# Attention on one core: the transposes of a head's sums stand behind the next head's second key block

## The reference, cut to what matters

```python
x = inputs.reshape(B, T, NUM_HEADS, HEAD_DIM).transpose(0, 2, 1, 3)
q = x * rotation_params[None, :, None, :]
k = x * entangle_params[None, :, None, :]
attn_scores = jnp.einsum('bhid,bhjd->bhij', q, k) / sqrt(16)
out = jnp.einsum('bhij,bhjd->bhid', softmax(attn_scores), x)
...
x = x + layernorm(attention(layernorm(x)))
x = x + layernorm(token_mixing_ffn(layernorm(x)))
x = x + layernorm(linear_attention_block(layernorm(x)))
x = x + layernorm(quantised_ffn(layernorm(x)))
```

## Time and profile before

| | |
|---|---|
| time, median of 3 runs | 3713.15 us (3712.55 to 3713.18) |
| the profiled execution: span | 3718.8 us (its own time is given only as this span) |
| TensorE matmul busy | 3322.9 us, 89% |
| ScalarE busy | 2477.6 us, 67% |
| VectorE busy | 1495.2 us, 40% |
| GpSimd busy | 214.5 us, 6% |
| TensorE's mean granted clock | 0.958 |
| DMA | 178.49 MB, mean 48 GB/s |

### The profile page before, as it was taken

One profiled execution on the slowest core, in us unless ns is written; L12 is line 12 of the kernel. 1 busy time (PEld: TensorE's weight loads), 2 busy tenths in 40 slices (PEclk: granted clock), 3 DMA queues, 4 the chain that ended last, 5 costly groups with the idle time before them and its releaser, 6 DMA issues. The chain is left out here.

```text
span 3718.8 us, 54135 instructions
## 1 busy us (share of the span) xinstructions
PE 3322.9 (89%) x18048; PEld 1368.4 (37%) x18049; DVE 1495.2 (40%) x3462; ACT 2477.6 (67%) x2634; POOL 214.5 (6%) x183
## 2 busy tenths in 40 slices
PE   1999999999999999999999966658888888889996
PEld 0222222222222222222222224435555666665664
DVE  5233211212201202202201026665677777765664
ACT  1998998998998998999999962223333333333332
POOL 0000000000000000000000001111111111111100
PEclk9999999999999999999999987879999999999998
DMA  6111111101101101101100011221111221110110
GB/s 208 62 36 35 55 32 37 51 29 44 52 31 40 46 31 48 48 30 48 39 31 31 31 26 51 74 59 49 46 51 51 62 68 51 51 48 33 45 35 23
DMA packets 122866, 178.49 MB, mean 48 GB/s; under 512 B 40016, under 2 KB 97616, under 8 KB 122320
## 3 DMA queue, kind: packets, MB, share of 16 engines
q1 hardware_dynamic: 122576, 174.75, 14.8%
HBM read 107.62 MB, written 67.11 MB: 47 GB/s over the span
## 5 line engine op out<-in xcount | busy, mean ns | idle before, releaser
L368 ACT ACTIVATE probs<-ps 128x1024 f32<-128x1024 f32 x2048 | 1982.8, 1021 | 182.2 <-PE ps L270 157.3
L328 PE MATMUL ps<-probs,vals 128*32 128x512 f32 x8192 | 1099.7, 609 | 19.7 <-issue 19.7
L270 PE MATMUL ps<-qT,kT 99*128 99x512 bf16 x4096 | 1072.3, 384 | 40.8 <-DMA kT<-split_dram 29.0
L270 PEld LDWEIGHTS ps<-qT,kT 99*128 99x128 bf16 x4096 | 318.7, 98 | 1134.6 <-ACT probs L368 843.5
L485 DVE COPY sums<-ps 128x512 f32<-128x512 f32 x64 | 44.3, 692 | 1324.0 <-PE ps L328 1324.0
L328 PEld LDWEIGHTS ps<-probs,vals 128*32 128x32 f32 x8192 | 161.8, 108 | 440.4 <-ACT probs L368 355.9
L750 PE MATMUL layers_ps<-weight_mem,hT 128*128 128x256 f32 x1024 | 232.9, 387 | 0.0
L744 PE MATMUL layers_ps<-yT,weight_mem 128*128 128x512 f32 x512 | 227.8, 597 | 2.6 <-ACT hT L983 2.6
L1010 ACT ACTIVATE gate<-layers_ps 128x512 f32<-128x512 f32 x96 | 57.3, 597 | 247.0 <-PE layers_ps L898 201.5
L750 PEld LDWEIGHTS layers_ps<-weight_mem,hT 128*128 128x128 f32 x1024 | 199.1, 196 | 29.1
L898 PE MATMUL layers_ps<-n4T,weight_mem 128*128 128x512 f16 x768 | 181.4, 393 | 30.9 <-DVE n4T L1233 23.4
(11 more groups left out here) (152 smaller groups left out, 2809.2 us busy)
## 6 DMA issues: line engine op xcount, KB each, us to landing
split_dram<-parts SPq DMA_DIRECT2D x32, 768.0 KB, 3.7
qT<-split_dram SPq DMA_DIRECT2D x64, 192.0 KB
kT<-split_dram SPq DMA_DIRECT2D x64, 192.0 KB
xs<-in_x_dram SPq DMA_DIRECT2D x4, 2048.0 KB, 16.2
qT<-split_dram SPq DMA_DIRECT2D x64, 128.0 KB
kT<-split_dram SPq DMA_DIRECT2D x64, 128.0 KB
heads_dram<-result SPq DMA_DIRECT2D x64, 128.0 KB, 7.4
attn<-heads_dram SPq DMA_DIRECT2D x16, 512.0 KB, 5.5
```

The source lines that it names most:

```text
L270: last = nc.tensor.matmul(SCORES[slot][:, n * BANK:(n + 1) * BANK], kT[buf][0:ROWS_QK, j * P:(j + 1) * P], qT[buf][0:ROWS_QK, q0:q0 + BANK ...
L328: mm = nc.tensor.matmul(ACC[32 * c:32 * c + 32, :], vals[buf][:, j, :], probs[:, j % PROBS, c * BANK:(c + 1) * BANK], start=(j == 0), stop ...
L368: nc.scalar.activation(probs[:, j % PROBS, half * T // 2:(half + 1) * T // 2], SCORES[slot_of(at)], ACT.Exp).then_inc(exps_done, 1)
```

## The change

The four transposes of a head's sums get a function of their own, `turn_sums`. They are issued in the next head, behind the products of its block 1 (`FINISH_AT`), with the wait for `sums_ready` ahead of them; the last head keeps them at its end. So that the first head can go without them, TensorE's loop now runs over groups 1 to 6, and group 0 is written out ahead of it.

```diff
+FINISH_AT = 1
...
+            def turn_sums():
+                for t in range(QC):
+                    last = nc.tensor.transpose(TURN[:, t * P:(t + 1) * P], sums[:, t * P:(t + 1) * P], ident[:, :])
+                last.then_inc(result_full, 1)
...
                         mm.then_inc(probs_free, 1)
+                        if j == FINISH_AT and not (isinstance(head, int) and head == 0):
+                            pe.wait_ge(sums_ready, head)
+                            turn_sums()
                         if j == ROUND_AT and e < ROUNDS and not last_group:
...
-                    pe.wait_ge(sums_ready, head + 1)
-
                     if last:
+                        pe.wait_ge(sums_ready, head + 1)
                         pe.wait_ge(result_read, head + 1)
-                    for t in range(QC):
-                        mm = nc.tensor.transpose(TURN[:, t * P:(t + 1) * P], sums[:, t * P:(t + 1) * P], ident[:, :])
-                    mm.then_inc(result_full, 1)
-
-            with pe.Fori(0, GROUPS - 1) as group:
+                        turn_sums()
+
+            group_of_heads(0, False)
+            with pe.Fori(1, GROUPS - 1) as group:
                 group_of_heads(group, False)
             group_of_heads(GROUPS - 1, True)
```

## The result

| | before | after |
|---|---|---|
| median, us | 3716.19 (6 runs, 3712.55 to 3720.31) | 3727.16 (6 runs, 3725.23 to 3731.48) |
| ratio to before, 95% interval | | 1.0031 (1.002 to 1.0043) |
| span of the profiled execution | 3718.8 | 3723.5 |
| its own time | not given | 3725.33 |

The change is slower by 0.3%, some 11 us. The forecast was 3708.6, with a range of 3700 to 3715. Of the nine executions of experiment 4's kernel two took 5912 and 6436 us, the profiled one among them, against 3720 to 3728 for the others; they are left out of its median and ratio, and the kernel was run once more for a profile.

What follows compares the result with a forecast made beforehand. TensorE was taken to bound the attention, with ScalarE following. The terms -1.1 + 2.8 - 5.2 - 1.0 summed to -4.5 us, from the median 3713.15 to 3708.6 us, range 3700 to 3715.

Steps and rivals of the forecast that it cites:

- What bounds the attention: Attention: TensorE is the bound at 1.96 us a key block, ScalarE follows; transposes cost about 0.5 us wherever they stand.
- Rival 1: Head ends: ScalarE is the bound and its holes close, 56 x 0.5 = 28 us, 3680; chance 0.05.
- rival 3: Group ends: the 3 us gap belongs to the group end, not the jump; running through saves nothing, 3714; chance 0.07.
- (a): 56 ordinary head ends: lose 0.51 us and gain 0.49 each, -1.1 us in all.
- (b): Next head's first products: wait for acc_free loses its cover, 0.05 us each, +2.8 us, ends 0 and +9.5.
- Rival 4: Block 0's products in every head: acc_free comes late, 0.35 us a head gives 3725, slower; chance 0.05.
- (c): First group end, run through without a jump: -5.96 + 0.8 for a possible low-clock spell, -5.2 us, ends -6.0 and -4.4.
- (d): Five remaining TensorE jumps, reached without waiting for the sums: -1.0 us, ends -1.0 and +2.5; clock spells unchanged, ±3.
- (e): VectorE's reciprocal and product and SyncE's store behind the transposes: some 3 us later, still covered, cost nothing.
- Rival 2: Five remaining jumps: shorter gap keeps TensorE's clock up, some 11 us beside the -4.5, 3697; chance 0.10.
- signs of being wrong: Head much under 16 x 1.96 + 0.5 us, block 0's products over 1.2 us behind scores, or first-group-end gap.

Runs made afterwards that it cites:

- experiment 4: Kernel before, nothing moved, with 44 semaphore increments at the start of TensorE's program: 3723.66 us, ratio 1.0025; run once more for a profile, ratio 1.0015.
- experiments 6 and 7: All eight groups written out on TensorE, no loop: changed kernel's order 3687.8 us, ratio 0.9922; order of the kernel before 3682.11 us, ratio 0.9915.
- Experiment 8: Changed kernel with TensorE's groups written out, block 0's products waiting for sums_ready in place of acc_free: 3683.06 us, ratio 0.9913.
- experiments 1 and 2: Changed kernel with semaphore increments at the start of TensorE's program: 24 of them 3709.42 us, ratio 0.9972; 8 of them 3726.05 us.
- experiment 1: Changed kernel with 24 semaphore increments at the start of TensorE's program: 3709.42 us, ratio 0.9972.
- experiments 6 to 11: Either order with TensorE's groups written out, 3687.8, 3682.11 and (wait on sums_ready) 3683.06 us; ScalarE's too, 3671.78, 3672.26 and (moved, direct wait) 3674.66 us.

## Why the prediction was wrong, point by point

- **What bounds the attention: right.** TensorE is the bound, its transposes cost about 0.49 us wherever they stand, and ScalarE's hole moved along unchanged. Rival 1 (28 us) is refuted, and so is rival 3: the 3 us gap goes with the jump (first group end of the changed kernel, and all seven in experiments 6 and 7).
- **(a) and (b), the ordinary heads: right.** Forecast -1.1 + 2.8 = +1.7, measured 0.04 to 0.05 a head, about +2.5. The delay was 0.06 us, put at 0.05. Experiment 8 shows that it is VectorE's handover in two steps. Rival 4 had this wait as its mechanism for the slower side: the side was right, the mechanism not.
- **(c), the group that is run through: right in what it removed.** The jump and the spell behind it were put at -5.96 and measured -6.0. The +0.8 for a new spell at this end did not come.
- **(d), the five jumps that stay: wrong, and this is the step that failed.** "If the jump takes as long as before, -0.2 each; if nothing is gained by being early, +0.5": both ends took it for granted that a jump is one stop whose length the program around it doesn't touch. Measured was +2.64 each, +13.2 in all. The part that I had weighed came as forecast: block 0's products start 5.18 us behind the last block's instead of 5.86, 0.7 sooner, with 0.49 paid again at block 1. What I had at nothing is a second stop, within block 0, because writing out group 0 moved the loop's head to some fifteen instructions ahead of the end of a stretch of code (six pairs of weight load and product and the waits ahead of them; by experiments 1 and 2 more than 8 and at most 24). No row of the kernel before shows that. The page of the Trainium skill that I cited for (c), "Runtime: NRT & Kernel Launch" (Instruction fetch mechanics), gives the stretches of 256 and the stall at a taken branch. It does not say that the target's place in its stretch counts, but from these two the question could have been asked, and I asked it for the jump that went and not for those that stayed.
- **(e), the work behind the transposes: right.** No new wait of L263 or of SyncE appears.
- **Rival 2 (clock): the other way.** The granted clock at the five jumps fell: one minus the clock, times the five stretches of time, is 22.3 us in the changed kernel against 13.8 before, and 15.5 with the second stop gone (experiment 1). Nor did the clock stay up there, though TensorE reached each jump sooner.
- **The sum and the range** took the remaining jumps at -1.0, ends -1.0 and +2.5, and nothing for the place of the loop's head. The sum with the measured values, +2.5 - 6.0 + 13.2 - 1.5, is +8.2 against a forecast of -4.5. With the head moved by 24 instructions the trace has -6.0, so the other terms held, in part by luck: 1.5 of it is the seventh end's spell. Of my signs of being wrong (a cheaper head, products over 1.2 us late, a gap at the first end) none came true, and none looked at a jump that stays.

## What to carry to other kernels

A diff that changes a loop's bounds or adds code ahead of a loop changes where its head lies in the fetched code, and this alone was worth 14 us here in the trace, more than all that the diff meant to do. Count it as a term of its own, and try a few instructions without effect ahead of the loop before judging such a change; or write the loop out, as experiments 6 to 11 did. And before moving work out of a hole, ask which engine is the bound: a hole on the engine that follows is only the picture of work on the one that leads.

## What the runs showed of the hardware that I had not expected

- A taken jump on TensorE stops it for 3.0 to 3.7 us in the kernel before. Where the target lies some fifteen instructions ahead of the end of a fetched stretch there is a second stop, and the jump costs 2.6 us more in all; with the target two products and two scores further ahead it is 4.3 us over six jumps, and the stop shrinks to some tenths in the profile at most of them.
- Eight increments at the start of the program move that stop by exactly four products, twenty-four remove it. The 256 instructions of a stretch are stated by the Trainium skill, "Runtime: NRT & Kernel Launch" (Instruction fetch mechanics); the runs fix the end of the stretch, not its length.
- Straight code is free here: eight groups written out, some 3,650 instructions each on TensorE by my count (3782 - 129, good to some tens), show no stop at any of the seven group ends but the one that ScalarE's table load causes.
- A handover in two steps on VectorE (wait for its own copy, then raise a semaphore) reaches TensorE 0.06 us later than a copy that raises it itself.
